# Context attention with queries, keys and probabilities split in rows and turned by DMA transfers in SBUF

## The reference

```python
q = (draft_hidden @ Wq.T).reshape(bsz, draft_len, H, HD)      # 16 heads of 128
q = _rms_norm(q, q_norm_w).transpose(0, 2, 1, 3)
kv_in = jnp.concatenate([context_hidden, draft_hidden], axis=1)
k = _rms_norm(..., k_norm_w)      # 4 heads of 128, from kv_in
v = ...                           # 4 heads of 128, from kv_in
q, k = _rope(q, draft_position_ids), _rope(k, full_position_ids)
scores = jnp.einsum('bhqd,bhkd->bhqk', q, k) * SCALE
probs = jax.nn.softmax(scores, axis=-1)
attn = jnp.einsum('bhqk,bhkd->bhqd', probs, v)
return attn @ Wo.T                # x = layernorm(x + this)
```

## Time and profile before

| | us |
|---|---|
| median of three runs | 3000.09 (2999.10 to 3002.46) |
| profiled execution | 3004.53 |
| span in the profile (first to last instruction) | 3002.7 |
| mean granted TensorE clock | 0.969 of full speed |
| the stage, first DMA issue to the first of the next stage | 464.65 to 1301.33 of the span |

### The profile page before, as it was taken

The page is one execution under the profiler, slowest core; times in us unless marked ns, Lnnn a source line. Parts: engine busy times, 40 slices in busy tenths (PEclk is TensorE's granted clock), DMA queues, the critical chain, the costliest instruction groups (busy, mean ns, idle before and its releaser), DMA issues. The chain is left out here.

```text
span 3002.7 us, 49266 instructions
## 1 busy us (share of the span) xinstructions
PE 2727.9 (91%) x17011; PEld 1595.3 (53%) x17276; DVE 1958.4 (65%) x3681; ACT 1574.4 (52%) x3629; POOL 1204.2 (40%) x1238
## 2 busy tenths in 40 slices
PE   6789896899999999959976998998889999999998
PEld 4677672555555555524434665666654444444443
DVE  5778896878787888767656788887463232322335
ACT  7999983655555555464417777676432221222121
POOL 3889885745454545224333111111142212222121
PEclk8999997999999999989997999999989999999999
DMA  4111103100000000040012000000021111111211
GB/s 161 40 54 48 43 33 120 43 5 8 4 7 4 7 4 4 1 168 1 1 50 74 19 19 18 14 16 19 12 90 65 45 50 63 63 63 32 65 32 67
DMA packets 50541, 122.53 MB, mean 41 GB/s; under 512 B 7042, under 2 KB 11522, under 8 KB 48163
## 3 DMA queue, kind: packets, MB, share of 16 engines
q1 hardware_dynamic: 50338, 120.00, 12.3%
HBM read 111.25 MB, written 4.52 MB: 39 GB/s over the span
## 5 line engine op out<-in xcount | busy, mean ns | idle before, releaser
L2060 POOL TENSOR_TENSOR s_state<-s_state,s_ct 128x512 f32<-128x512 f32 x256 | 326.8, 1302 | 82.0 <-DVE s_state L2235 79.6
L2235 DVE TENSOR_TENSOR_SCAN s_state<-s_decay,s_psd 128x512 f32<-128x512 f32 x256 | 301.8, 1208 | 68.3 <-PE s_psd L2380 34.7
L1044 DVE TENSOR_TENSOR m_prod<-m_bank,m_gated 128x512 f32<-128x512 f32 x88 | 60.8, 691 | 437.6 <-ACT m_gated L853 437.6
L779 POOL TENSOR_TENSOR m_aTl<-m_prod,m_aTh 128x512 bf16<-128x512 f32 x88 | 101.8, 1157 | 584.0 <-ACT m_aTh L855 584.0
L853 ACT ACTIVATE m_gated<-m_bank 128x512 f32<-128x512 f32 x88 | 52.5, 597 | 437.3 <-PE m_bank L1166 437.3
L1156 PE MATMUL m_bank<-m_xTl,m_wh 128*128 128x512 bf16 x704 | 267.8, 380 | 3.1 <-ACT m_wh L819 1.0
L1155 PE MATMUL m_bank<-m_xTh,m_wh 128*128 128x512 bf16 x671 | 255.5, 381 | 2.4 <-DVE m_prod L1044 2.4
L2380 PE MATMUL s_psd<-ident,s_v 128*128 128x128 f32 x1024 | 166.0, 287 | 41.8 <-DVE s_state L2235 21.1
L2136 ACT ACTIVATE s_decay<-s_dt,s_nega 128x508 f32<-128x508 f32 x256 | 181.6, 710 | 20.4 <-DVE s_state L2235 20.3
L2149 ACT ACTIVATE s_v<-s_uT,s_bT 128x512 f32<-128x512 f32 x256 | 182.1, 712 | 0.8 <-PE s_psd L2380 0.7
L2380 PEld LDWEIGHTS s_psd<-ident,s_v 128*128 128x128 f32 x1024 | 123.1, 147 | 88.6 <-ACT s_v L2149 47.1
(11 more groups left out here) (516 smaller groups left out, 8070.2 us busy)
## 6 DMA issues: line engine op xcount, KB each, us to landing
s_ct<-ssm_bc SPq DMA_DIRECT2D x64, 256.0 KB, 3.2
m_scale<-moe_scale SPq DMA_DIRECT2D x64, 256.0 KB, 3.2
m_stage<-in_moe_w_dram SPq DMA_DIRECT2D x16, 768.0 KB, 5.0
m_stage<-in_moe_w_dram SPq DMA_DIRECT2D x8, 864.0 KB, 7.8
X<-in_x_dram SPq DMA_DIRECT2D x4, 1024.0 KB, 12.2
a_cf<-in_ctxT_dram SPq DMA_DIRECT2D x16, 256.0 KB, 2.7
a_wstage<-in_xa_wq_dram SPq DMA_DIRECT2D x8, 512.0 KB, 3.6
a_wstage<-in_xa_wo_dram SPq DMA_DIRECT2D x8, 512.0 KB, 4.0
```

The costliest lines, as they stand in the source:

```text
L2060: pool.tensor_tensor(h, h, ct[t % 4][:, s * P:(s + 1) * P].unsqueeze(1).broadcast_to([P, KB, P]), ALU.mult).then_inc(weighted, 1)
L2235: dve.tensor_tensor_scan(state[i % RING][:, :], decay[t % 2][:, s, :, :].rearrange("p m t -> p (m t)"), ps_d[i % 2][:, :], 0.0, ALU.mult, ...
```

## The change

Queries, keys and probabilities are split into their parts before they are turned, in the layout in which they lie (rows are tokens), and both parts are turned together by DMA transfers from SBUF to SBUF. `a_rotp` holds a chunk's two parts, `a_pp` the two parts of the probabilities of a group; `a_kT`, `a_qT` and `a_pT` are where the transfers write. A transfer moves 128 x 1024 values of bf16, 256 KB; in a pass there are 6 for chunks and 8 for probabilities. ACT makes the high parts (`turned_high`, `prob_high`), POOL the low parts of a chunk (`turned_low`), DVE those of the probabilities (`prob_low`), with the reciprocal multiplied in on the way, so that `a_prob` is no longer rewritten. The two PSUM tiles `a_pst` go to the chunks, which rotate over four `a_psp` tiles. SP now follows the whole pass, all 16 of them written out.

```diff
+            def turn_chunks(n, g, j):          # SP
+                for c in (2 * g - 2, 2 * g - 1):
+                    r = c % 2
+                    sp.wait_ge(t_low.sem, t_low.at(n, c + 1))
...
+                    sp.dma_start(out, rotp[r][:, :, :].rearrange("p a n -> p (a n)"), transpose=True).then_inc(t_done[r].sem, 16)
+
+            def turn_probs(s, g):              # SP
+                for a, ready, done in ((0, p_high, ph_done), (1, p_low, pl_done)):
+                    sp.wait_ge(ready.sem, ready.at(s, g + 1))
+                    if a == 0 and (g or late(s, 1)):
+                        sp.wait_ge(pv.sem, pv.at(s, g) if g else pv.at(s - 1))
+                    sp.dma_start(pT[:, a, :, :, :].rearrange("p k h q -> p (k h) q"),
+                                 pp[:, a, :, :, :].rearrange("p k h t -> p (k h t)"), transpose=True).then_inc(done.sem, 16)
...
+            def turned_low(n, c):              # POOL
+                pool.wait_ge(t_high.sem, t_high.at(n, c + 1))
+                pool.tensor_tensor(rotp[c % 2][:, 1, :], rot[c % 2][:, :], rotp[c % 2][:, 0, :], ALU.subtract).then_inc(t_low.sem, 1)
...
+            def turned_high(n, c):             # ACT
+                act.wait_ge(roped.sem, roped.at(n, 2 * c + 2))
+                if c >= 2 or late(n, 1):
+                    act.wait_ge(t_done[r].sem, ...)
+                act.activation(rotp[r][:, 0, :], rot[r][:, :], ACT.Copy).then_inc(t_high.sem, 1)
...
             def prob_high(s, g):
-                for k in range(2):
-                    act.wait_ge(p_turned.sem, p_turned.at(s, 2 * g + k + 1))
-                    act.activation(pTh[:, k, :], ps_t[k][:, :], ACT.Copy).then_inc(p_high.sem, 1)
+                act.wait_ge(rtot.sem, rtot.at(s, g + 1))
...
+                for h in range(GH):
+                    e = act.activation(pp[:, 0, :, h, :], prob[:, h, :]..., ACT.Copy, scale=rtotal[:, h:h + 1])
...
             def turn(s, p, start=None, last=False, last_x=False):   # ACT
                 for g in range(4):
-                    if g:
-                        prob_high(s, g - 1)
+                    if g and not last:
+                        turned_high(s + 1, 2 * g - 2)
                     exponentials(s, g, p)
                     if not last:
                         chunk(s + 1, 2 * g, 1 - p)
+                    prob_high(s, g)
+                    if g and not last:
+                        turned_high(s + 1, 2 * g - 1)
...
-                for h in range(GH):            # DVE, normalize
-                    m = dve.tensor_scalar(prob[:, h, :], prob[:, h, :], rtotal[:, h:h + 1], None, ALU.mult)
...
             def prob_low(s, g):
-                    dve.tensor_tensor(pTl[:, k, :], ps_t[k][:, :], pTh[:, k, :], ALU.subtract).then_inc(p_low.sem, 1)
+                for h in range(GH):
+                    m = dve.scalar_tensor_tensor(pp[:, 1, :, h, :], prob[:, h, :]..., rtotal[:, h:h + 1], pp[:, 0, :, h, :],
+                                                 ALU.mult, ALU.subtract)
...
-                    for k in range(4):         # PE, turn_chunks
-                        mm = pe.transpose(ps_t[r][:, k * P:(k + 1) * P], rot[r][:, k * P:(k + 1) * P], fr.ident[:, :])
-                for k in range(2):             # PE, turn_probs
-                    for h in range(GH):
-                        mm = pe.transpose(ps_t[k][:, h * P:(h + 1) * P], prob[:, h, k * P:(k + 1) * P], fr.ident[:, :])
...
             def values(s, g, p):
-                pe.wait_ge(p_low.sem, p_low.at(s, 2 * g + 2))
+                pe.wait_ge(ph_done.sem, ph_done.at(s, 16 * g + 16))
+                pe.wait_ge(pl_done.sem, pl_done.at(s, 16 * g + 16))
```

More of the change, by code:

```diff
@@ L1252, in stage_xattn @@
         woh, wol = (fr.sb(f"a_wo{n}", [P, 16, D], BF16, st) for n in "hl")
-        ln = LayerNorm(fr, st, "a")
+        wstage = [fr.sb(f"a_wstage{j}", [P, 1024], F32, st)[:, :] for j in range(3)]
+        ln = LayerNorm(fr, st, "a", r=wstage[2][:, 0:D])
         xs = fr.sb("a_xs", [P, D], F32, st)
@@ L1330, in stage_xattn @@
         v_low = Count(fr, "a_vlow", 2)
-        turned = Count(fr, "a_turned", 6)
+        t_done = [Count(fr, f"a_tdone{r}", 48) for r in range(2)]
         t_high = Count(fr, "a_thigh", 6)
@@ L1376, in _ @@
             wl.sync(sp, wlow, 4, first_wo)
-            context(2)
-            wl.sync(sp, wlow, first_wo)
-            with sp.Fori(3, SEQS) as s:
-                context(s)
+            turn_chunks(0, 1, 0)
+            wl.sync(sp, wlow, first_wo, first_wo + 3)
+            turn_chunks(0, 2, 0)
+            turn_chunks(0, 3, 0)
+            turn(0, 0, start=0)
+            for s in range(1, SEQS - 2):
+                turn(s, s % 2)
+            turn(SEQS - 2, 0, last_x=True)
+            turn(SEQS - 1, 1, last=True, last_x=True)
         @block.gpsimd
@@ L1469, in _ @@
             c_low_part(1, 1)
-            for g in range(3):
+            for g in range(4):
+                if g:
+                    turned_low(0, 2 * g - 2)
+                    turned_low(0, 2 * g - 1)
                 if g == 1:
@@ L1811, in values @@
                     cols = slice(g * HD, (g + 1) * HD)
-                    mm = three(pe, ps_v[:, :], (vh[p][:, k, cols], vl[p][:, k, cols]), (pTh[:, k, :], pTl[:, k, :]), k == 0, k == 1)
+                    mm = three(pe, ps_v[:, :], (vh[p][:, k, cols], vl[p][:, k, cols]), [pT[:, a, k, :, :].rearrange("p h q -> p (h q)") for a in range(2)], k == 0, k == 1)
                 mm.then_inc(pv.sem, 1)
@@ L1825, in turn @@
                     scores(s, g, p)
-                    if g:
-                        turn_probs(s, g - 1, t_low.at(s) if g == 1 or last else t_low.at(s + 1, 2 * g - 2))
-                    elif start != 0:
-                        turn_probs(s - 1, 3, t_low.at(s))
                     if not last:
```

165 lines of the change are left out of this document (74 added, 91 removed).

## The result

| | before | after |
|---|---|---|
| median | 3001.28 us (2999.10 to 3004.52, 4 runs) | 3085.15 us (3083.26 to 3087.13, 4 runs) |
| ratio | | 1.0279, 95% interval 1.0261 to 1.0296 |
| profiled execution: span | 3002.7 us | 3085.3 us |
| pass 0, pass 1 | 49.9, 48.0 us | 58.4, 57.0 us |
| passes 2 to 13, mean | 48.8 us | 52.9 us |

A forecast was written before the change was run, and what follows sets the result against it. PE was taken as the bound: a steady pass of 48.7 - 6.2 + 3.8 + 0.7 = 47.0, plus a 1.6 us clock fall, 48.6. With the ends, about +9 us on 3000.1 gave 3010; range 2979 to 3100.

The forecast's parts named there:

- rival 2: On SP's queue: transposing transfers dearer than plain ones set the pace; 3035 us, or 3045 to 3120; chance 0.32.
- PE gains 6.2 us a pass: On PE: 56 transposes of 0.11 us leave each pass, taking it from 48.7 to 42.5 us before waits.
- None of the three becomes the bound by its sum. What matters is the order in which they serve the new path.: On ACT, DVE and POOL: their total work would not set the pace, only their order toward the transfers would.
- POOL's chain: On POOL in group 1: second key chunk scaled by 5.9 us, low part, angles, low part of chunk 1 by 13.4.
- The low parts like the multiplications, 0.39: On DVE: the 16 fused low-part operations a pass priced like the earlier multiplications, 0.39 us each.
- The wait of group 1, 3.8 us, behind POOL's angles: At PE's values of group 1: transfers queue behind chunk 1, late from POOL's angles; landing 18.1 against 14.3, wait 3.8 us.
- Groups 0, 2 and 3: 0.7 us in all: At PE's values: group 3 waits 0.7 us after its table load; groups 0 and 2 wait about nothing.
- One clock fall a pass, 1.6 us: On PE: the 3.8 us wait lowers the granted clock once a pass, costing 1.6 us; steady pass 48.6.
- The ends: Stage's first and last passes: pass 0 +7, pass 1 +5, pass 14 -5.5, pass 15 0; +3 for more clock falls.
- rival 3: In the transfers: each row a packet of 0.117 us, 7.5 us a transfer; about 3870 us; chance 0.06.

The follow-up runs named there:

- e7_plain_low: Changed kernel with the probabilities' low parts made by a plain multiplication, leaving the subtraction out (wrong in value): 3064.94 us, against 3085.15 for the changed kernel.
- e4_filler: Changed kernel with useless products on PE ahead of its wait for the probabilities in groups 0, 1 and 3: 3083.94 us, against 3085.15 for the changed kernel.
- the run of 2992 us: Only queries and keys turned by transfers, probabilities still on PE, POOL's angles moved to group 0: 2992.08 us, ratio 0.9942 to the kernel before.

## Why the prediction was right and wrong

The sign, slower, was right and the time lay in the range (3085 in 2979 to 3100); the forecast of 3010 was 75 us short. That the range held is luck: only the dearer end of rival 2 reached 3085, and it did so for a cause that the runs refute. By the prediction's own steps:

- *PE gains 6.2 us a pass.* Right, and of no use while PE waits: to products of 42.5 us, by the forecast's prices, come 8.0 us of waits, and the low clock fills the rest of the 52.9.
- *"None of the three becomes the bound by its sum. What matters is the order in which they serve the new path."* **This step failed.** No engine is full, DVE ended at 73%; but at the forecast's prices its work would be some 29.5 us a pass (39 less eight subtractions and six of chunks at 0.68), and it measured 38.4. And I followed the order only along the path to the transfer, and never asked when DVE comes to the next maxima. DVE lost the work that filled its wait for the exponentials (2.6 us a pass more of it) and its wait for x's high part (3.0 us, new); the maxima, and with them the exponentials, came when DVE's row was through. This row, work and waits together, makes the steady pass, shown by the slope of `e7_plain_low` (1.6 us for 1.8), by the nothing that clock and transfers bring, and by the 3.2 us that its order, with POOL's, gives back. That the 3.0 us for x's high part count in full is argued from the sum of DVE's pass. The prediction had ACT's four high parts ahead of it as 1.3 us, and used them only for POOL's chain.
- *The low parts like the multiplications, 0.39.* Too low by half: 0.77 in place of 0.39, 16 x 0.38 = 6.1 us a pass on the engine that sets the pace. It is the largest single mis-sized term; the 4.1 us by which the pass grew would be gone without it if the slope of `e7_plain_low` held that far, which wasn't tried.
- *The wait of group 1, 3.8 us, behind POOL's angles.* 4.9, there and by that chain, but a symptom. With SP's order changed it moves and the pass stays. That the same low part also holds up DVE's chunk 3 was missed: `a_rot` has two halves, and the wait was in the code. The angles in group 0 bring 1.8 us.
- *Groups 0, 2 and 3: 0.7 us in all.* 1.45 at the values of group 0 and 1.25 or 2.15 at those of group 3, so about 8.0 in all in place of 4.5. I had DVE's and ACT's steps too cheap (ACT's four high parts 1.7 for 1.3, the transfer 3.2 for 2.7 and 1.29 for 0.33), and had the group start where PE does.
- *One clock fall a pass, 1.6 us.* The clock fell (0.95) and the run with the filled waits (1.00, a pass of 52.8 for 52.9) shows that it cost nothing. Here PE was not the one waited for. The profile gives the clock as a share only. What the share does to a product can be read from the trace of before: at 0.50 two products of 512 columns start 0.43 us apart, at 1.00 0.21:

```profile
534.58 0.63 PE L1870 MATMUL a_psv<-a_pTl,a_vh 128*128 128x512 bf16 x1
535.01 0.63 PE L1871 MATMUL a_psv<-a_pTh,a_vl 128*128 128x512 bf16 x1
...
538.04 0.38 PE L1870 MATMUL a_psp<-a_wql,a_xTh 128*128 128x512 bf16 x1
538.25 0.38 PE L1871 MATMUL a_psp<-a_wqh,a_xTl 128*128 128x512 bf16 x1
```

  That is about 1.2 and 2.4 columns a ns, an estimate from these rows, and this is what the prediction and the expectation of `e4_filler` call 1.2 and 2.4 GHz.
- *Rival 2, the dearer transfer.* Its sign was measured, SP rows of 1.29 us and landings of 3.2, and its time for 2.0 us a transfer (3060 to 3085) is what came. Its prices of 1.5, 2.0 and 2.5 us had no row behind them. At the price that was measured it would have given no more than 3035. It would have been easy to call it the cause. It isn't: plain copies, at 0.55 and 2.4 us, leave the pass at 52.8. The transposing form landed 0.8 us later than a plain copy of the same bytes and held SP 0.7 us longer; why, no run shows.
- *The ends.* Passes 0 and 1 +8.5 and +9.0 for +7 and +5 (+3). Pass 14 -0.2 for -5.5, since I took it that only the angles made a wait. Pass 15 and behind it +8.3 for 0: PE waits 5.2, 1.8 and 4.7 us at the values of its last three groups, with nothing beside them, where before it waited 2.07. Plain copies take 4.4 us off this part.

## To carry to other kernels

When work is taken from the leading engine, ask for each other engine not only how full it is but when it comes round to the step that starts the next group: work that left a gap in its row, a new wait, and work that came behind it, all push that step back. A wait of the old bound shows where the delay arrives, not where it is made; to find out, change the price of one thing at a time and look at the slope of the pass, and add up one engine's pass, work and waits, before and after. And turn by DMA first what is read a group or more later: the queries and keys did it for free (PE busy 559.90 of 560 us in the run with passes of 45.5), the probabilities have not yet paid.

## What the runs showed of the hardware

- *The low part has no single price.* Four of them take 3.46 us at 910.98, where POOL adds and scales a tile beside them, and 1.67 in pass 15, where POOL is idle:

```profile
1324.78 1.67 DVE L1705 SCALAR_TENSOR_TENSOR a_pp<-a_prob,a_rtotal,a_pp 128x256 bf16<-128x256 f32 x4 [1.77 <-ACT a_pp L1588]
```

  The plain multiplications of `e7_plain_low` take 3.02 and 2.04 us for four in groups 0 and 1, and 1.14 in pass 15. Those of the kernel before went from 1.14 to 1.77 in the group with the angles; the prediction did not look at that row. That DVE and POOL hinder each other is argued from these rows: pass 15 lacks other work too, and no run took POOL's work away from the steady passes.
- *A transfer that turns 256 KB in SBUF* held SP 1.29 us and landed after 3.2; the same as a copy 0.55 and 2.4. The two of a group that were issued at 940.63 and 942.0 landed 3.3 and 3.2 us later, about 1.3 apart, where the prediction had 1.0 for each behind another. The queue's packets rose from 50338 to 286882 for 224 transfers, about 1056 each, which is near the 1024 of one for each row of 128 values; they took 22.1% of the engines against 12.3, so 0.021 us each, where rival 3 had 0.117 for every packet. From the same shares (17.6% with plain copies) a turning transfer keeps the 16 engines busy for 1.4 us and a copy for 0.77, an estimate from rounded shares.
- *The stages behind are not quite the same from kernel to kernel.* From the last layer norm of this stage to the first load of the experts' weights it is 887 us before (1299.1 to 2186.5), 895 after, and 908 in the run of 2992 us (1268.9 to 2176.5), with the granted clock at 0.98 in stretches where it was 1.00 before. The code of those stages is the same. Of the 30 and 37 us that the stage gains in the two runs with queries and keys alone and the angles in group 0, the stages behind take back 18 and 16, and the cause stays open.
